# A convolution by row transform: 13 products over 7 arrays in place of 14 over 11, and a new order of all calls

## The reference

```python
k = conv(x, w1, padding=6, rhs_dilation=2) + b1
k = conv(k, w2) + b2                       # 1x1, 49 channels
attn = softmax(k, axis=1)
out0 = einsum('bkchw,bkhw->bchw', shifts(xpad), attn)
y = gelu(yc[None, :, None, :] + out0 * D)  # yc: scan of 64 steps
o = layernorm_over_channels(out0 + y) * ln_w + ln_b
```

## Time and profile before

| | us |
|---|---|
| median of 3 runs | 800.34 (799.68 to 800.49) |
| profiled execution | 799.94, its span 797.8 |
| TensorE busy | 744.9 (93%) |
| VectorE busy | 673.8 (84%) |
| ScalarE busy | 546.9 (69%) |
| GpSimd busy | 193.8 (24%) |

### The profile page before, as it was taken

How to read it: one execution, slowest core, us unless ns; L and a number is a source line. 1 busy time by engine, 2 the same in 40 slices (tenths; PEclk the granted TensorE clock), 3 DMA queues, 4 the chain that set the end, 5 groups by cost and what they waited for, 6 DMA issues and landing times.

```text
span 797.8 us, 27596 instructions
## 1 busy us (share of the span) xinstructions
PE 744.9 (93%) x12338; PEld 446.7 (56%) x12338; DVE 673.8 (84%) x867; ACT 546.9 (69%) x903; POOL 193.8 (24%) x115
## 2 busy tenths in 40 slices
PE   4959989999999999999999999999999999999994
PEld 1525545675557545664567545664567545764681
DVE  0898997989889988989888988989888988686675
ACT  2874454757686786867686786687786677486566
POOL 5114113024311243024311341114301431013010
PEclk9969999999999999999999999999999999999998
DMA  9482223023714146224705255324704230414124
GB/s 298 134 140 34 42 54 56 2 42 55 150 27 94 28 86 116 55 43 79 145 6 95 40 105 83 72 35 86 133 3 94 45 78 3 92 28 71 28 55 106
DMA packets 266721, 58.60 MB, mean 73 GB/s; under 512 B 266265, under 2 KB 266346, under 8 KB 266346
## 3 DMA queue, kind: packets, MB, share of 16 engines
q1 hardware_dynamic: 138488, 40.79, 24.1%
q10 hardware_dynamic: 128114, 16.04, 13.0%
HBM read 40.04 MB, written 16.78 MB: 71 GB/s over the span
## 4 chain that ended last, share of the span: by engine, by line
PE 28%; DVE 21%; ACT 19%; issue 12%; ACTq 3%; POOL 3%; DVEq 0%; POOLq 0%
PE cv L526 15%; PE wk L575 7%; ACT V L913 5%; ACT chs L967 4%; DVE V L1435 3%; ACTq L957 3%; DVE o L1583 2%; POOL chs L417 2%; DVE tg L1577 2%; DVE Z L1476 2%; PE ms L606 2%; PE wk L596 2%; ACT tg L1002 2%; PE wk L634 1%; DVE Z L1485 1%
## 5 line engine op out<-in xcount | busy, mean ns | idle before, releaser
L526 PE MATMUL cv<-V,W 128*32 128x496 f16 (+6 forms) x7840 | 429.0, 374 | 6.3 <-issue 4.1
L526 PEld LDWEIGHTS cv<-V,W 128*32 128x32 f16 (+1 forms) x7840 | 198.3, 96 | 205.0 <-issue 18.2
L913 ACT ACTIVATE V<-R,sc 128x1024 f16<-128x1024 f32 (+1 forms) x88 | 109.9, 1277 | 61.6 <-DVE R L1361 50.3
L386 POOL TENSOR_TENSOR R<-raw 128x1152 f32<-128x1152 f32 x32 | 94.5, 2954 | 203.8 <-DVE V L1435 105.1
L1435 DVE SCALAR_TENSOR_TENSOR V<-R,sc,V 128x1024 f16<-128x1024 f32 (+1 forms) x88 | 115.1, 1327 | 3.0 <-ACT V L913 3.0
L596 PE MATMUL wk<-band,XT 128*128 128x209 f16 (+1 forms) x1080 | 87.7, 238 | 3.3 <-ACT o L989 3.0
L596 PEld LDWEIGHTS wk<-band,XT 128*128 128x128 f16 x1080 | 78.6, 97 | 15.0 <-ACT o L989 8.4
L575 PEld LDWEIGHTS wk<-AT,sel 128*128 128x128 f16 x2268 | 69.6, 100 | 15.0 <-issue 7.8
L411 POOL TENSOR_TENSOR chs<-o 128x1024 f32<-128x1024 f32 x14 | 45.2, 3226 | 130.0 <-DVE o L1583 121.0
L575 PE MATMUL wk<-AT,sel 128*128 128x16 f16 (+1 forms) x2268 | 73.9, 190 | 0.1
L1361 DVE SCALAR_TENSOR_TENSOR R<-R 128x1024 f32<-128x1024 f32 (+1 forms) x56 | 68.6, 1257 | 0.0
(11 more groups left out here) (194 smaller groups left out, 909.8 us busy)
## 6 DMA issues: line engine op xcount, KB each, us to landing
raw<-in_x_dram SPq DMA_DIRECT2D x16, 1024.0 KB, 11.5
out_dram<-o SPq DMA_DIRECT2D x28, 512.0 KB, 4.6
AT<-in_x_dram ACTq DMA_DIRECT2D x82, 128.0 KB, 3.0
w1raw<-in_L_conv_w_dram SPq DMA_DIRECT2D x2, 3136.0 KB, 16.7
xs<-in_x_dram ACTq DMA_DIRECT2D x40, 128.0 KB, 3.0
out_dram<-o SPq DMA_DIRECT2D x8, 256.0 KB, 3.9
AT<-in_x_dram SPq DMA_DIRECT2D x4, 128.0 KB, 3.0
xs<-in_x_dram SPq DMA_DIRECT2D x2, 128.0 KB, 3.6
```

The lines of the kernel that those rows point to most:

```text
L386: nc.gpsimd.tensor_tensor(R[buffer][:, :, :, :], rows_of(par, j + 2), rows_of(par, j), ALU.subtract).then_inc(pool_rows, 1)
L526: ins = pe.matmul(to.rearrange("p (w t c) -> p w t c", w=2, c=COLS)[:, :, :, c0:c1], W[:, ws, h * K7 + v, k0:k1], slot(n, a)[:, low, :, t0 ...
L913: nc.scalar.activation(v_array(n, a, 0), array(a), ACT.Identity, scale=sc[:, par, 3:4]).then_inc(vhi, 1)
```

## The change

The transform gets other points: taps 0 to 3 of the rows use 0, 1, -1, 2, -2, 1/2 and infinity, taps 4 to 6 all of these but infinity. Both parts now read the same arrays: 7 arrays a unit instead of 11 (six of 9 windows, one of 8) and 13 products instead of 14. Six blocks have two products and block 4 has one, with the 10 matmuls of `SINGLE` a step. VectorE makes four row arrays e0 to e3 from x, then u1, u2, and from these the points 1 and -1; GpSimd makes six differences (g2, g0, g1, g3, h1, h3) in place of four, g from the e arrays and h from x; in unit 0 VectorE makes all six itself. The logits get four additions of the product at 1/2 (`logits_a`) in place of `logits_d`, with three more scales. Two weight sets get five more sums (`point_sums`); only five of the seven rows are copied as they are. The bank rotation fits the new blocks, and all calls on TensorE, VectorE, ScalarE and GpSimd stand in a new order. SP's list stays.

```diff
-ARRAYS = 11
-ARRAY_WINS = (8, 8, 8, 8, 8, 8, 8, 8, 9, 9, 8)
-ROW_STEPS, POOL_ROWS = 17, 4
+ARRAYS = 7
+ARRAY_WINS = (9, 9, 9, 9, 8, 9, 9)
+ROW_STEPS, POOL_ROWS = 17, 6
-BLOCKS = (((M1P, 0, 0, 0), (M1M, 1, 1, 0)), ((M1P, 2, 2, 0), (M1M, 3, 3, 0)),
-          ((M2P, 4, 4, 0), (M2M, 5, 5, 0)), ((M2P, 6, 6, 0), (M2M, 7, 7, 0)),
-          ((M0, 8, 8, 0), (MD, 8, 9, 0)), ((M0, 9, 10, 1), (MI, 8, 11, 1)), ((M0, 9, 9, 0), (MI, 10, 12, 0)))
+BLOCKS = (((M1P, 0, 0, 1), (M1M, 1, 1, 1)), ((M1P, 0, 2, 0), (M1M, 1, 3, 0)),
+          ((M2P, 2, 4, 1), (M2M, 3, 5, 1)), ((M2P, 2, 6, 0), (M2M, 3, 7, 0)), ((MI, 4, 8, 0),),
+          ((M0, 5, 9, 1), (MA, 6, 10, 1)), ((M0, 5, 11, 0), (MA, 6, 12, 0)))
-SLOT_FREE = (-3, -1, 0, 0, 1, 1, 2, 2, 3, 3, 4)
+SLOT_FREE = (-3, -2, 0, 0, 2, 2, 4)
+SINGLE = ((X, 0, "A0", 0), (X, 1, "A1", 0), (X, 2, "B0", 0), (X, 3, "B0", 1),
+          (X, 0, "A2", 0), (X, 1, "A0", 1), (X, 2, "B1", 1), (X, 3, "B1", 0), (X, 0, "A1", 1), (X, 1, "A2", 1))
...
+            def make_e(n, par, j, wins):
+                if n:
+                    dve.wait_ge(row_made, ROW_STEPS * n)
+                for h in range(HALVES):
+                    nc.vector.scalar_tensor_tensor(out=R[j][:, 0:wins, h, :], in0=rows_of(par, j, wins)[:, :, h], scalar=-POINT,
+                                                   in1=rows_of(par, j + 1, wins)[:, :, h], op0=ALU.mult,
+                                                   op1=ALU.add).then_inc(row_made, 1)
+            def make_e0(n, par):
...
+                else:
+                    for h in range(HALVES):
+                        dve.wait_ge(first_in[h], 16)
+                make_e(n, par, 0, 10)
...
+            def logits_a(n, par):
+                add_sum(n, par, zrow(0), MA, zrow(0), ALU.add, 13)
+                for k in range(1, 4):
+                    add_sum(n, par, zrow(k), MA, zrow(k), ALU.add, 13, scale=7 + k)
```

```diff
+            make_e0(0, 0)
+            make_e1(0, 0)
+            make_e2(0, 0)
+            make_e3(0, 0)
+            make_u1(0)
             row_sums(0, 6)
             row_sums(0, 2)
             row_sums(0, 5)
             row_sums(0, 3)
-            row_sums(0, 1)
-            make_u1(0, 0)
-            make_u0(0, 0)
+            make_u2(0)
+            make_x1_plus(0)
+            row_sums(0, 1)
             row_sums(1, 6)
...
```

ScalarE's `unit` in the stretch of `apply`:

```diff
                 attended(m, other, 0)
                 attended(m, other, 1)
                 attended(m, other, 2)
+                gelu(m, 0, 0)
                 fetch_rows(n, 0)
                 fetch_rows(n, 1)
+                attended(m, other, 3)
+                attended(m, other, 4)
+                gelu(m, 0, 1)
+                attended(m, other, 5)
                 fetch_rows(n, 2)
                 if nxt:
                     v_high(n + 1, other, 0)
...
```

TensorE's `unit` at the same place:

```diff
+                conv(n, 30, 33)
                 apply(m, 0)
                 apply(m, 1)
                 apply(m, 2)
+                conv(n, 33, 35)
                 apply(m, 3)
                 apply(m, 4)
                 apply(m, 5)
-                conv(n, 30, 33)
                 apply(m, 6)
                 apply(m, 7)
-                mean(m, 0)
+                conv(n, 35, 36)
                 turn_x(n, par, 0)
                 turn_x(n, par, 1)
+                mean(m, 0)
```

More of the change, by code:

```diff
@@ L514, in conv @@
                         if b == 4:
-                            pe.wait_ge(z_step, ZSTEPS * n + 3)
+                            pe.wait_ge(z_step, ZSTEPS * n + 1)
                         if b == 5:
                             pe.wait_ge(z_step, ZSTEPS * n + 4)
-                    begun, left = set(), {(g, t): ROUNDS_LEFT[g, t] for g in (X, Y) for t in range(4)}
-                    for g, t, kind, later in ROUNDS:
+                    rounds = BLOCK_ROUNDS[b]
+                    begun, left = set(), {(g, t): sum(1 for r in rounds if r[:2] == (g, t)) for g in (X, Y) for t in range(4)}
+                    for g, t, kind, later in rounds:
                         total, a, ws, t0 = BLOCKS[b][g]
@@ L534, in conv @@
                         ins.then_inc(conv_done, 1)
-            ROUNDS_LEFT = {(g, t): sum(1 for r in ROUNDS if r[:2] == (g, t)) for g in (X, Y) for t in range(4)}
             def turn_logits(m, w):
@@ L1090, in unit @@
+                gelu(m, 1, 1)
                 spread_mean(m, 0)
-                gelu(m, 1, 1)
-                table_of_ln()
-                turned_x(n, par, 0)
                 fetch_rows(n, 3)
                 square(m, 0, 0)
-                turned_x(n, par, 1)
+                square(m, 0, 1)
                 fetch_rows(n, 4)
-                square(m, 0, 1)
+                if nxt:
+                    v_high(n + 1, other, 1)
+                table_of_ln()
+                fetch_rows(n, 5)
@@ L1614, in unit @@
                     normalise(m - 1, 1, 1)
+                fold_1(n, par)
                 softmax_divide(m)
+                v_low(n, par, 4)
                 attention_low(m)
-                make_y2_minus(n)
-                make_q2(n)
-                v_low(n, par, 6)
-                v_low(n, par, 7)
+                make_xa(n)
+                if nxt:
+                    scales(n + 1, other)
+                logits_1(n, par)
+                v_low(n, par, 5)
+                if nxt:
+                    make_e0(n + 1, other)
+                    make_e2(n + 1, other)
+                    logit_scales(n + 1, other)
@@ L1750, in weight_scales @@
                 dve.wait_ge(s_wscale, 4)
-                for column, factor in enumerate((1.0, -1 / 6, 1 / 6, 1 / 24, 1 / 48, -1 / 48, 0.25), start=3):
+                for column, factor in enumerate(POINT_FACTORS, start=3):
                     nc.vector.tensor_scalar(wsc[:, column:column + 1], wsc[:, 2:3], W_SCALE * factor, None,
@@ L1879, in _ @@
             m = UNITS - 1
-            logits_i(m, 1)
             logits_0(m, 1)
+            logits_a(m, 1)
             def last_shift(w):
```

583 lines of the change are left out of this document (290 added, 293 removed).

## The result

The changed kernel takes 836.1 us (835.27 to 837.49, 4 runs) against 800.41 for the kernel before: ratio 1.0448, 95% interval 1.043 to 1.0467. The prediction said 825, within 790 to 842, slower. The profiled execution took 835.69 us, span 833.7, 35.9 more than before.

A forecast was written before the change was run, and what follows sets the result against it. TensorE, busy 86.4 of 88.4 us in a middle unit, was taken to set the period. Start +17, unit 0 +0.5, units 1 to 6 +10, unit 7 -2 made +25.5: 825 us, range 790 to 842.

The forecast's parts named there:

- Part 3, the start: Before block 0: row sums queue behind the wait for x, e0 to e3 and u1; +17 us, lower bound +9.6.
- Part 3, unit 0: Unit 0: VectorE takes over GpSimd's differences, TensorE idles before blocks 2 and 5, block 4 gives 3 back; +0.5 us.
- Part 1: Convolution block 4 holds one product, 10 matmuls a step instead of 20: gain 3.0 us a unit.
- Part 2: Elementwise work of a unit: VectorE's sum falls by 1.2 us, ScalarE saves about 4.5, GpSimd gets two more differences.
- rival 3: GpSimd's long instructions block VectorE's SBUF instructions: +4.3 us a unit, 841 to 843 in all; chance 0.12.
- Part 4, units 1 to 6: New order, walked through four engine programs: new waits 7.0 less gains 4.8, +2.2 us; +1.6 taken, six units +10.
- (a): In apply: `apply(5)` waits 2.1 us for `attended(3)`, behind gelu(0,0) and two fetches on ScalarE, and 0.4 after it.
- (b): `turn_x(2)` waits 1.2 us for `turned_x_low(0)`, now behind both centres, two row sums and `logits_i`.
- (c): Unit's end: `turn_x(6)`, `(7)` and the next block 0 wait 1.5 us together, `turn_logits(0)` about 1.5.
- (d): The band: band_low(0) stands behind e0, e2 and five scales on VectorE; 0 to 1.0 us, taken 0.3.
- 1: Rival: units become TensorE-bound at last, period 84.9 us, 786 to 793 in all; chance 0.22.
- 2: Rival: the start costs its 17 us and the units nothing, new waits eating just the 4.8; 817; chance 0.18.

The follow-up runs named there:

- a1: The changed kernel with VectorE's row sums of half 0 back at the head, ahead of e0 to e3: 822.3 us, ratio 1.0275.
- b1: The kernel before, with VectorE waiting for both halves of x before its first row sum: 811.0 us, ratio 1.0137.
- c3: The changed kernel with ScalarE's second bound moved behind the turned attention and VectorE's scales behind e2: 823.9 us, ratio 1.0287.
- a3: The changed kernel with 20 matmuls instead of 10 in each step of block 4 (that product is wrong): 847.8 us, ratio 1.0573.
- d4: d1 with 20 matmuls instead of 10 in each step of block 4 (that product is wrong): 819.6 us, ratio 1.0231.
- c1: The changed kernel with GpSimd's six differences a unit done on one element each (arrays wrong): 835.8 us, ratio 1.0437.
- d3: d1 with GpSimd's six differences a unit done on one element each (arrays wrong): 807.7 us, ratio 1.0088.
- d1: The changed kernel with the moves of c4 and c3 together: 808.7 us, ratio 1.0095.
- d2: d1 with TensorE's variance and second mean later, ScalarE's deviation behind V high 2 and 3, first bound behind the first exponentials: 855.9 us, ratio 1.0683.
- c4: a1 with unit 0's two-part point sums and V low 4 moved behind the weight sets block 2 waits for: 820.3 us, ratio 1.0231.

## Why the prediction was right, and where it was short

The direction, the size of the start and the period were right; the sum of +25.5 was 10.4 short of 35.9, and 836.1 lies above the 818 to 835 that the forecast gave for itself.

**Part 3, the start.** +17 predicted, +18.0 measured: the first row sum came at 36.46 ("near 37"), block 0 at 73.80 ("near 73"). a1 and b1 show that the cause is the one named, for 14.3 of the 18.0 us; the 3.7 that stay in a1 are not in the prediction's terms. The upper bound was the right choice over the +9.6 of the work list: the first row sum came 16.4 us late and block 0 18.0, so the chain behind it had no slack.

**Part 3, unit 0.** The +0.5 failed: +4.0. The idle times were near the forecast (3.7 before block 2 for 5; 2.0 before block 5 for 2), though the first was for a weight set, not for arrays. What the sum left out is the clock: it was counted at block 0 in words only. TensorE did 70 matmuls fewer in unit 0, 3.0 us by part 1, and yet was busy 60.0 us against 59.3, at a mean clock of 0.91 for 0.97: some 3.6 us of clock, about all of the difference of 3.5 to the forecast. Part of that is chance of the execution. In c3 the same idle time before the same matmuls left the clock at 1.00, and they took 4.37 us instead of 6.05:

```profile
123.63 4.37 PE L539 MATMUL cv<-V,W 128*32 128x512 f16 x80 [2.04 <-DVE ev L1504]
```

**Part 1.** 4.36 us for the 70 matmuls (4.5 predicted), TensorE's unit 2.6 to 2.7 shorter for a predicted 3.0. Right in work. In time the same product is worth 1.5 to 1.9 a unit in a3 and 1.4 to 1.6 in d4: the step counted all of it as gain on the path.

**Part 2.** VectorE's sum was to fall by 1.2 and rose by 0.5. The groups by shape of the unit 501 to 591 tell why:

```profile
L1352 DVE SCALAR_TENSOR_TENSOR R<-R 128x1152 f32<-128x1152 f32 x7 | 10.8, 1560 | 0.0
L1459 DVE SCALAR_TENSOR_TENSOR V<-R,sc,V 128x1152 f16<-128x1152 f32 x6 | 10.6, 1785 | 1.0 <-ACT V L927 1.0
```

Their means are 1560 and 1785 ns for 1351 and 1407 in the earlier trace rows: 1.5 and 2.3 us of stalls beside GpSimd. c1 and d3 say that this cost no time in either order, so leaving it out of the sum was right, and rival 3 (+4.3 a unit) is refuted in its mechanism although the total, 836, lay near its 841 to 843.

**Part 4, units 1 to 6.** Predicted +10 (the walk gave 2.2 a unit, 1.6 was taken), measured +11.2, period +2.25. The total was right in part by luck, as its parts were not:
- (a) `apply(5)` waits 1.0 to 1.2, not 2.1, and the 0.4 behind it is absent. ScalarE's timeline of the changed kernel in `apply`, which begins at 460.52:

```profile
466.53 0.37 ACTq L971 DMA_DIRECT2D xs<-in_x_dram  x1
...
466.93 0.61 ACTq L971 DMA_DIRECT2D xs<-in_x_dram  x1
467.63 1.69 ACTq L971 DMA_DIRECT2D AT<-in_x_dram  x2
469.37 1.33 ACT L1003 ACTIVATE o<-wk,sc 128x512 f32<-128x512 f32 x2 [1.42 <-PE wk L607]
```

The four issues took 2.8 us, not the 3.5 of the earlier trace rows, and run beside gelu's table load and activation: `attended(3)` is done 9.5 us after the first apply, not 10.6.
- (b) `turn_x(2)` waits 0.56, not 1.2.
- (c) The unit's end: the next block 0 waits 0.3 to 0.5 for V low 1, `turn_logits` does not wait at all (1.5 predicted). In its place `mean(m, 1)` waits 1.05 for the residual, and `variance` 1.5 for GpSimd, where the sum had the old waits of 1.8 as gone.
- (d) The band waits 0.8, not 0.3, and the cause was another.
- Not in the walk: both `bound` calls at the head of ScalarE's list, in front of V high 2, with a wait for x of 2.3 us. By c3 the second call alone, 1.9 us of work, is worth 2.0 a unit, or 12 us; what the first and the wait cost is open. It was in the change and I read past it: I hadn't asked what stands behind each moved call. The single waits I had over-estimated made up for it.

**Unit 7 and the tail.** -0.2 for -2, and +2.9 for nothing. TensorE's timeline at the end of the last convolution of the changed kernel, and the windows table of the tail, before and after:

```profile
773.06 1.97 PE L617 MATMUL ms<-chs,ones 128*64 128x512 f32 x4 [4.55 <-POOL chs L433]
```

```profile
735.40:797.80 62.40, 47.29 (x562) 32.95 (x561) 43.53 (x74) 36.35 (x56) 6.60 (x5) 0.92 0.27 60
```

```profile
768.40:833.70 65.30, 48.57 (x565) 33.19 (x561) 46.48 (x78) 36.66 (x55) 7.42 (x5) 0.90 0.25 55
```

The last variance waits 4.55 us for squares, where the kernel before waited 1.54 there and 1.32 behind it, and the 5.5 us after it run at clock 0.50 (0.73 in 5.5 us before). In the tail TensorE is idle 1.6 us longer and busy 1.3 us longer with as many matmuls: together the 2.9. This is read from the traces; no run tested it.

**Rivals.** 1 (units TensorE-bound): of the versions that compute everything d1 and c3 have the best units, 88.6 a period, still 3.7 above the 84.9 it asked for. 2 falls with the period, 4 with the start. No version here beats the kernel before: d1 is 0.7 to 1.2% slower. Open is whether another order would turn the 4.8 us of idle time in d1's units into time; d2's moves together did the opposite. Untested too is an earlier load of x: ScalarE still stands 2.50 us for it in d1's unit.

## What to carry to other kernels

When calls are reordered, write down for each what it waits for and what stands behind it in its engine's list: one maximum of 1.9 us in front of the call that the next block needs cost 2.0 us a unit here, as much as the saved product gave, and in d2 a call put first in its list stood for 10.5 us, with work behind it that used to fill this time. Work removed from the bounding engine is a gain only as far as no wait takes it; here 2.6 us of matmuls were worth 1.4 to 1.9. A stall that is plain in the trace can be free: take it away in a run before building on it.

## What was not expected of the hardware

- An idle time of TensorE of 2 to 4 us can cost 1.4 to 1.7 us on top of itself. After 3.65 us of idle time in d2 the granted clock was 0.64 over the next 4 us, in unit 0 after 3.68 us it was 0.76 over the next 7.1, after 2.04 us 0.72 over 6. It isn't certain: after 2.04 us in c3, 2.34 in c4 and 2.48 in one unit of d2 the clock stayed at 1.00 over the next 6 us, while after only 1.51 us in d2 (at 594.77) it was 0.68 over 4. The waits of up to 1.7 us in the changed kernel's units 1 to 7 left it at 1.00. What decides is open.
- A low half of V (1.41 us alone) took 3.55 us beside two differences on GpSimd.
- Four DMA issues on ScalarE's queue took 2.8 us in all while an activation ran beside them.
